# One DMA per channel index over all 128 partitions, in place of one DMA per image over 64

## The chip, the cores and the metric

The kernel runs on one core of one Trainium2 chip. The metric is the time of one execution in microseconds (us) on the device. Three executions of the kernel before took 1348.41, 1350.67 and 1353.38 us; their median is 1350.67 us.

## The reference

The input x is float32 of shape (32 images, 384 channels, 64, 64). Each channel group is normalised, displaced by an integer offset that belongs to one of 48 positions (8 channels each), filtered by a 5x5 Gaussian with the fraction of the offset, and added to x:

```python
def _gn(v, G=32, eps=1e-5):          # 32 groups of 12 channels
    g = v.reshape(B_, G, C_ // G, H_, W_)
    return ((g - mean(g)) / sqrt(var(g) + eps)).reshape(v.shape)

off_round = round(offset)             # (48, 2)
disp = displace(x.reshape(B, P, cpp, h, w), off_round)   # zero outside the image
sub = offset - off_round
kernel = exp(-sum((grid + sub)**2) / (2 * 0.5**2)); kernel /= sum(kernel)   # 5x5 for each position
out = depthwise_conv(disp, kernel, padding=2)

x = x + conv_ref(_gn(x), offset)
```

Displacement and filter are separable, so the kernel applies both as two matrix products, one along the rows of an image and one along its columns.

## The kernel before, in words

**Tiles.** A step handles 2 images (B) and 24 channels (SUPER). 16 steps (STEPS) go over the 32 images; 16 superblocks (NSUPER) go over the 384 channels. That is 256 steps of 768 KB each way. A tile `xin[:, s]` has 128 partitions: partition 2*(16*a + m) + b holds lane a (one of 4 channels), four image rows (block m of 16), image b. Its free axis has 6 channel indices q (Q) of 256 elements, 1 KB each. So one image has the even partitions and the other the odd ones. `xin` has 16 slots, one for each step of a superblock.

**Engines in one step t.** SyncE (queue SP) loads x into slot s. VectorE (DVE) takes the statistics ten steps ahead of use (`statistics`, L395), and adds the result into `xin` (`add_x`, L411 and L414). GpSimd (POOL) makes mean and scale. ScalarE (ACT) normalises the tile of step t + 1 into `norm` (two instructions, L498), copies `y` of step t out of PSUM (one instruction, L507), and then issues the store of step t - 2 (L523). TensorE (PE) multiplies along the rows (`yp`, L572), and along the columns one step later (`xp`, L591).

**Order.** Every engine has its own program in a fixed order, and semaphores tie them. On ACT the order is `normalise(t + 1)`, `copy_y(t)`, `store(t - 2)`, and in 5 of the 16 steps of a superblock one more activation behind the store (L476 twice, L480, L487 twice), which prepares the matrices of the next superblock. `copy_y(t)` waits for `y_done`, that is for the last L572 matmul of step t. `y_products(t + 1)` on PE waits for `y_ready`, that is for `copy_y(t)`, since there is one `yp` buffer, and for `norm_ready` of its step. The DMAs of a store are issued by ACT's own sequencer, so they stand in the same program as the activations.

**Loops.** The first and the last superblock are written out; the 14 between them are one hardware loop, whose body is 16 steps. In the loop each DMA is preceded by register work for its address.

**Loads.** SP waits for `stored[s]`, the completion of both DMAs of the store of this slot, and then issues the load of the same slot for the next superblock. Each DMA adds 16 to its semaphore.

Of the kernel before, what the change touches and what calls it, by code (L numbers as in the profile page):

```python
# [11 lines left out]
P = 128  # L12
POSITIONS = 48
B = 2
LANES = 4
R = 4
BLOCKS = HW // R
SUPER = 24
NSUPER = CH // SUPER
Q = SUPER // LANES  # L20
# [23 lines left out]
def displaced_conv(nc: bass.Bass, x: bass.AP, offset: bass.AP, out: bass.AP):  # L44

    def tiled(a):
        return a.rearrange("(m b) (s q a) (h r) w -> m b s (a h) q (r w)", b=B, s=NSUPER, q=Q, a=LANES, r=R)

    x_t, out_t = tiled(x), tiled(out)
    off_row = offset.rearrange("(o p) k -> o (p k)", o=1)  # L50

    with ExitStack() as ctx:
        def sb(name, shape, dt=F32):
            return ctx.enter_context(nc.sbuf_tensor(name, shape, dt))

        def sem(name):
            return ctx.enter_context(nc.semaphore(name))


        xin = sb("xin", [P, SLOTS, Q, ROW])  # L60
# [66 lines left out]
        loaded = [sem(f"loaded{i}") for i in range(SLOTS)]  # L127
        stored = [sem(f"stored{i}") for i in range(SLOTS)]
# [36 lines left out]
        def run(step):  # L165

            def superblock(c, head=False, tail=False):
                for s in range(STEPS):
                    step(c, s, head, tail)
            superblock(0, head=True)  # L170
            with nc_engine[0].Fori(1, NSUPER - 1) as c:
                superblock(c)
            superblock(NSUPER - 1, tail=True)
# [3 lines left out]
        @block.sync  # L177
        def _(sync):
            sync.dma_start(off[:, :, :], off_row.to_broadcast([P, 2 * POSITIONS])).then_inc(off_loaded, 16)

            def load(c, s):
                for b in range(B):
                    sync.dma_start(xin[b:P:B, s], x_t[s, b, c]).then_inc(loaded[s], 16)

            for s in range(SLOTS):
                load(0, s)
            with sync.Fori(1, NSUPER) as c:
                for s in range(SLOTS):
                    sync.wait_ge(stored[s], 16 * B * c)
                    load(c, s)  # L190
            for s in range(SLOTS):
                sync.wait_ge(stored[s], 16 * B * NSUPER)

        @block.gpsimd
        def _(pool):
# [91 lines left out]
        def _(dve):  # L287
# [101 lines left out]

            def statistics(c, s, n, pair=None):  # L390
                if n == 0:
                    dve.wait_ge(loaded[s], 16 * B * (c + 1))
                if pair is not None:
                    dve.wait_ge(stat_summed, pair - 3)
                nc.vector.bn_stats(stats[:, s // 2 % 4, s % 2, n, :],  # L395
                                   xin[:, s].rearrange("p (g q) f -> p q f g", g=GROUPS)[:, n]).then_inc(bn_done, 1)
# [20 lines left out]
            for s in range(QUAD):  # L417
                for part in range(CHUNKS):
                    statistics(0, s, part)
# [6 lines left out]
            for s in range(QUAD, 2 * QUAD):  # L426
                for part in range(CHUNKS):
                    statistics(0, s, part)
            for s in range(2 * QUAD, AHEAD):
                for part in range(CHUNKS):  # L430
                    statistics(0, s, part, pair=4 if part == 0 and s == 2 * QUAD else None)
# [33 lines left out]
        @block.scalar  # L465
        def _(act):
            nc_engine[0] = act
            act.wait_ge(taps_sq, 1)
            nc.scalar.activation(tap_sq[:], tap[:], ACT.Square).then_inc(taps_sq, 1)
            act.wait_ge(taps_sq, 2)  # L470
            nc.scalar.activation(tap_e[:], tap_sq[:], ACT.Exp, scale=-2.0).then_inc(taps_exp, 1)

            def square(c, part):
                source, target = ((t_int, t_isq), (t_full, t_fsq))[part]
                act.wait_ge(dist_ready, 2 * c + part + 1)
                nc.scalar.activation(target[:], source[:], ACT.Square).then_inc(sq_ready, 1)  # L476

            def exponential(c):
                act.wait_ge(sq_ready, 2 * c + 2)
                nc.scalar.activation(t_exp[:], t_fsq[:], ACT.Exp, scale=-2.0).then_inc(exp_ready, 1)  # L480

            def fill_rows(c, part):
                if part == 0:
                    act.wait_ge(made, c + 1)
                    if c is not 0:
                        act.wait_ge(mats_ready, MATS * c)
                nc.scalar.activation(next_ay[:].rearrange("p n r (m b) -> p n (r m) b", b=B)[:, :, :, part],  # L487
                                     t_msk[:, :, 0:R].rearrange("p n r m -> p n (r m)"), ACT.Identity,
                                     scale=same[:, part:part + 1]).then_inc(next_ay_ready, 1)

            def normalise(t, s, quad, g, first):
                if g == 0:
                    act.wait_ge(coef_ready, quad + 1)
                    if not first:
                        act.wait_ge(y_done, t - 1)
                cv, col = s // QUAD % 2, GROUPS * (s % QUAD) + g
                cols = slice(QG * HW * g, QG * HW * (g + 1))
                nc.scalar.activation(norm[:, s % 2, :, cols].rearrange("p r (q w) -> p q r w", w=HW),  # L498
                                     xin[:, s, QG * g:QG * (g + 1)].rearrange("p q (r w) -> p q r w", w=HW),
                                     ACT.Identity, bias=bias[:, cv, col:col + 1],  # L500
                                     scale=rstd[:, cv, col:col + 1]).then_inc(norm_ready, 1)

            def copy_y(t, v, first):
                act.wait_ge(y_done, t + 1)
                if not first:
                    act.wait_ge(x_done, ADDS * (t - 1))
                nc.scalar.activation(y[:, v].rearrange("p k r a m -> p a (k r) m"),  # L507
                                     yp[:, :, 0:POS * P].rearrange("p a (n m) -> p a n m", m=32),
                                     ACT.Copy).then_inc(y_ready, 1)

            square(0, 0)
            square(0, 1)
            exponential(0)
            act.wait_ge(filled, FILLS)
            for part in range(B):
                fill_rows(0, part)
            for g in range(GROUPS):
                normalise(0, 0, 0, g, True)

            def store(c, s, t):  # L520
                act.wait_ge(result_ready, ADDS * (t + 2))
                for b in range(B):
                    act.dma_start(out_t[s, b, c], xin[b:P:B, s]).then_inc(stored[s], 16)  # L523

            def step(c, s, head, tail):
                t = STEPS * c + s
                nxt = (s + 1) % STEPS
                q_next = QUAD * c + (s + 1) // QUAD
                if not (tail and s == STEPS - 1):
                    for g in range(GROUPS):  # L530
                        normalise(t + 1, nxt, q_next, g, head and s == 0)
                copy_y(t, s % 2, head and s <= 1)
                if s >= BEHIND:
                    store(c, s - BEHIND, t - BEHIND)
                elif not head:
                    store(c - 1, s - BEHIND + STEPS, t - BEHIND)
                if not tail:
                    if 4 <= s < 6:
                        square(c + 1, s - 4)
                    if s == 6:  # L540
                        exponential(c + 1)
                    if 10 <= s < 10 + B:
                        fill_rows(c + 1, s - 10)
            run(step)
            for s in range(STEPS - BEHIND, STEPS):
                store(NSUPER - 1, s, TOTAL - STEPS + s)
# [99 lines left out]
```

## Time and profile before

| | |
|---|---|
| median of three executions | 1350.67 us |
| profiled execution, its own time | 1354.66 us |
| its span, first to last instruction | 1352.8 us |
| mean granted clock of TensorE | 0.992 |
| busy: PE, DVE, ACT, POOL | 90%, 73%, 70%, 20% |
| DMA: bytes, packets | 403.14 MB, 409771 |

The profile shows one execution. A busy time counts the work of an engine, not that of its sequencer: register instructions and the issuing of DMAs stand apart, in rows whose engine has a q behind its name (ACTq, SPq). A duration in such a row is the time that the issuing sequencer was held; the data move later, in the 16 DMA engines. A bracket behind a row of the timeline gives the idle time before it and what ended it.

### The profile page before, as it was taken

The page shows a single profiled execution, that of the slowest core. Times are in us where ns is not written, and L with a number is a line of the kernel's source. Part 1 is how long each engine was busy: PE and PEld are TensorE (multiplying, and loading weights), DVE is VectorE, ACT ScalarE, POOL GpSimd, SP SyncE. Part 2 cuts the span into 40 slices and gives each one's busy share as a digit, 9 for nine tenths or more (in the row PEclk, how much of TensorE's full clock was granted, in tenths as well). Part 3 has the DMA queues.
Part 4 walks back from the last instruction along what each step waited for, and adds up shares of the span by engine and source line. Part 5 has one row for each costly group of instructions (what it writes and reads, how often), then busy time and mean ns, then how long its engine had stood idle before and what let it go on. Part 6 is the DMA issues. An engine that isn't in the chain of part 4 may idle for free.

```text
span 1352.8 us, 110317 instructions
## 1 busy us (share of the span) xinstructions
PE 1213.8 (90%) x49408; PEld 1142.0 (84%) x49408; DVE 991.2 (73%) x1530; ACT 942.3 (70%) x851; POOL 274.3 (20%) x646
## 2 busy tenths in 40 slices
PE   0888999999999999999999999999999999999897
PEld 0788888888898888888888888888888888888787
DVE  7667677777777777777777777777777777777543
ACT  3566776767777677776767777677777767777464
POOL 3211222122121211212121222212212122121010
PEclk9989999999999999999999999999999999999899
DMA  9589899999999999999999999999999999999745
GB/s 313 160 265 314 271 309 311 314 314 315 318 301 316 314 316 308 318 307 320 308 313 316 313 311 320 301 324 310 310 320 306 311 313 318 318 311 309 234 164 187
DMA packets 409771, 403.14 MB, mean 298 GB/s; under 512 B 16528, under 2 KB 409744, under 8 KB 409744
## 3 DMA queue, kind: packets, MB, share of 16 engines
q1 hardware_dynamic: 204944, 201.41, 48.2%
q10 hardware_dynamic: 204800, 201.36, 44.0%
q8 instruction: 18, 0.29, 0.1%
q14 instruction: 9, 0.07, 0.0%
HBM read 201.38 MB, written 201.33 MB: 298 GB/s over the span
## 4 chain that ended last, share of the span: by engine, by line
PE 89%; issue 7%; DVE 2%; ACT 0%; POOL 0%; ACTq 0%; POOLq 0%; DVEq 0%
PE yp L572 56%; PE xp L591 29%; PE xp L557 4%; DVE stats L395 1%; ACT y L507 0%; DVE xin L414 0%; ACT norm L498 0%; ACT next_ay L487 0%; POOL grid_i L200 0%; ACTq L523 0%; DVE t_msk L372 0%; DVE ay L382 0%; DVE tap_sum L358 0%; DVE tap_inv L361 0%; DVE sub L338 0%
## 5 line engine op out<-in xcount | busy, mean ns | idle before, releaser
L572 PE MATMUL yp<-ay,norm 32*128 32x128 f32 x24576 | 766.4, 276 | 66.8 <-ACT y L507 44.8
L572 PEld LDWEIGHTS yp<-ay,norm 32*128 32x128 f32 x24576 | 718.1, 188 | 89.9 <-issue 82.4
L507 ACT ACTIVATE y<-yp 128x1536 f32<-128x1536 f32 x256 | 371.5, 1451 | 310.5 <-PE yp L572 310.3
L498 ACT ACTIVATE norm<-xin,bias,rstd 128x768 f32<-128x768 f32 x512 | 496.9, 1018 | 53.4 <-issue 43.3
L395 DVE BATCH_NORM_STATS2 stats<-xin 128x6 f32<-128x512 f32 x768 | 508.4, 692 | 0.0
L591 PE MATMUL xp<-ax,y 64*64 64x64 f32 x24576 | 421.0, 221 | 9.6 <-issue 8.8
L591 PEld LDWEIGHTS xp<-ax,y 64*64 64x64 f32 x24576 | 384.8, 135 | 41.5 <-issue 10.9
L411 DVE TENSOR_TENSOR xin<-xp,xin 128x512 f32<-128x512 f32 x256 | 176.9, 691 | 321.6 <-PE xp L591 321.6
L414 DVE TENSOR_TENSOR xin<-xp,xin 128x1024 f32<-128x1024 f32 x256 | 309.4, 1208 | 12.2 <-PE xp L591 12.2
L241 POOL TENSOR_TENSOR stats<-stats 128x12 f32<-128x12 f32 x128 | 27.0, 211 | 986.6 <-DVE stats L395 980.0
L258 POOL TENSOR_TENSOR rstd<-var,mhalf 128x8 f32<-128x8 f32 x64 | 104.9, 1639 | 5.0
L557 PE MATMUL xp<-stats,ones 128*128 (+1 forms) x256 | 53.2, 292 | 56.4 <-POOL stats L241 29.0
L557 PEld LDWEIGHTS xp<-stats,ones 128*128 128x128 f32 x256 | 39.1, 192 | 73.1 <-issue 59.1
L487 ACT ACTIVATE next_ay<-t_msk,same 128x768 f32<-128x768 f32 x32 | 32.4, 1017 | 13.6 <-issue 7.7
L220 POOL TENSOR_TENSOR t_int<-grid,place 128x960 f32<-128x960 f32 x16 | 28.7, 1796 | 7.0 <-DVEq L354 7.0
L226 POOL TENSOR_TENSOR t_full<-t_int,sub 128x960 f32<-128x960 f32 x16 | 28.7, 1796 | 2.5 <-POOL t_int L220 2.3
L403 DVE TENSOR_REDUCE both<-xp 128x12 f32<-128x36 f32 x128 | 23.8, 186 | 4.9 <-PE xp L557 4.9
L382 DVE COPY ay<-next_ay 128x512 f32<-128x512 f32 x48 | 17.5, 422 | 12.2 <-PE yp L572 11.2
L476 ACT ACTIVATE t_isq<-t_int 128x960 f32<-128x960 f32 x16 | 16.1, 1004 | 8.1 <-issue 5.8
L476 ACT ACTIVATE t_fsq<-t_full 128x960 f32<-128x960 f32 x16 | 16.1, 1003 | 4.6 <-issue 3.7
L372 DVE SCALAR_TENSOR_TENSOR t_msk<-t_isq,t_exp 128x960 f32<-128x960 f32 x16 | 18.4, 1149 | 0.0
L480 ACT ACTIVATE t_exp<-t_fsq 128x960 f32<-128x960 f32 x16 | 16.0, 1003 | 2.9 <-issue 2.8
(52 smaller groups left out, 105.9 us busy)
## 6 DMA issues: line engine op xcount, KB each, us to landing
xin<-in_x_dram SPq DMA_DIRECT2D x512, 384.0 KB, 5.4
out_dram<-xin ACTq DMA_DIRECT2D x512, 384.0 KB, 4.2
off<-in_L_conv_offset_dram SPq DMA_DIRECT2D x1, 48.0 KB, 3.2
```

Source lines behind the costliest of these rows:

```text
L220: pool.tensor_tensor(t_int[:], grid[:, None, :, :].to_broadcast([P, POS, KINDS, HW]), place[:, bass.ds(POS * c, POS), :].unsqueeze(3).to_b ...
L258: pool.tensor_tensor(rstd[:, v], var[:, v], mhalf[:, :], ALU.pow).then_inc(small, 1)
L395: nc.vector.bn_stats(stats[:, s // 2 % 4, s % 2, n, :], xin[:, s].rearrange("p (g q) f -> p q f g", g=GROUPS)[:, n]).then_inc(bn_done, 1)
L411: nc.vector.tensor_tensor(at, xp[:, 2:4, 0], at, ALU.add).then_inc(result_ready, 1)
L414: nc.vector.tensor_tensor(at, xp[:, 0:2], at, ALU.add).then_inc(result_ready, 1)
L476: nc.scalar.activation(target[:], source[:], ACT.Square).then_inc(sq_ready, 1)
L487: nc.scalar.activation(next_ay[:].rearrange("p n r (m b) -> p n (r m) b", b=B)[:, :, :, part], t_msk[:, :, 0:R].rearrange("p n r m -> p n ...
L498: nc.scalar.activation(norm[:, s % 2, :, cols].rearrange("p r (q w) -> p q r w", w=HW), xin[:, s, QG * g:QG * (g + 1)].rearrange("p q (r w ...
L507: nc.scalar.activation(y[:, v].rearrange("p k r a m -> p a (k r) m"), yp[:, :, 0:POS * P].rearrange("p a (n m) -> p a n m", m=32), ACT.Cop ...
L557: nc.tensor.matmul(xp[:, 3, 1, 0:2 * GROUPS * 9], ones[:, :], stats[:, bass.ds(j, 1)].rearrange("p v t g s -> p (v t g s)"), start=True, s ...
L572: last = nc.tensor.matmul(yp[:, a, P * k:P * (k + 1)], norm[rows, v, r, P * k:P * (k + 1)], ay[rows, k, r, :], start=(r == 0), stop=(r == ...
L591: last = nc.tensor.matmul(xp[outs, 2 * (k // 2) + h, k % 2, HW * r:HW * (r + 1)], y[rows, v, k, r].rearrange("p a m -> p (a m)")[:, outs], ...
```

## The change

Each step's load and store is cut along the channel index q instead of the image b. Before there were two DMAs, each of one image: 64 partitions by 6 channel indices by 1 KB (384 KB, 384 rows of 1 KB). Now there are six DMAs, each of one channel index: 128 partitions by 1 KB (128 KB, 128 rows of 1 KB). The bytes, the size of a row and the slots stay the same. The semaphore counts follow: `stored` and `loaded` rise by 16 * 6 for each step instead of 16 * 2.

```diff
     def tiled(a):
-        return a.rearrange("(m b) (s q a) (h r) w -> m b s (a h) q (r w)", b=B, s=NSUPER, q=Q, a=LANES, r=R)
+        return a.rearrange("(m b) (s q a) (h r) w -> m s q (a h) b (r w)", b=B, s=NSUPER, q=Q, a=LANES, r=R)
...
             def load(c, s):
-                for b in range(B):
-                    sync.dma_start(xin[b:P:B, s], x_t[s, b, c]).then_inc(loaded[s], 16)
+                for q in range(Q):
+                    sync.dma_start(xin[:, s, q], x_t[s, c, q]).then_inc(loaded[s], 16)
...
-                    sync.wait_ge(stored[s], 16 * B * c)
+                    sync.wait_ge(stored[s], 16 * Q * c)
...
-                    dve.wait_ge(loaded[s], 16 * B * (c + 1))
+                    dve.wait_ge(loaded[s], 16 * Q * (c + 1))
...
             def store(c, s, t):
                 act.wait_ge(result_ready, ADDS * (t + 2))
-                for b in range(B):
-                    act.dma_start(out_t[s, b, c], xin[b:P:B, s]).then_inc(stored[s], 16)
+                for q in range(Q):
+                    act.dma_start(out_t[s, c, q], xin[:, s, q]).then_inc(stored[s], 16)
```

On ACT, in steps 4 and 5 of the first superblock, the program before has two DMAs of shape 64x6x256 between the copy of `y` and the activations that follow:

```order
L507 ACTIVATE y<-yp 128x4x12x32
L523 DMA out_dram<-xin 64x6x256 x2
L476 ACTIVATE t_isq<-t_int 128x960
L498 ACTIVATE norm<-xin,bias,rstd 128x3x4x64 x2
L507 ACTIVATE y<-yp 128x4x12x32
L523 DMA out_dram<-xin 64x6x256 x2
L476 ACTIVATE t_fsq<-t_full 128x960
```

At the same place the changed program has six of shape 64x2x256:

```order
L507 ACTIVATE y<-yp 128x4x12x32
L523 DMA out_dram<-xin 64x2x256 x6
L476 ACTIVATE t_isq<-t_int 128x960
L498 ACTIVATE norm<-xin,bias,rstd 128x3x4x64 x2
L507 ACTIVATE y<-yp 128x4x12x32
L523 DMA out_dram<-xin 64x2x256 x6
L476 ACTIVATE t_fsq<-t_full 128x960
```

No activation moved against another; each `norm` pair now stands behind four more issues.

On SP, the start of the program and of its loop, before and now (ISA is the register work of an address; the first of them also holds the wait for the slot):

```order
 L179 DMA off<-in_L_conv_offset_dram 128x96
-L183 DMA xin<-in_x_dram 64x6x256 x32
+L183 DMA xin<-in_x_dram 128x1x256 x96
 L187 UNCONDITIONAL_BRANCH
 L187 ISA
 L183 ISA
```

The 16 first loads are 96 DMAs instead of 32. In both loops, SP's and ACT's, each of the added DMAs brings an ISA row of its own. PE's and DVE's programs are the same row for row.

## Rows read from the trace of the kernel before

**Rows 1.** The page, part 1: busy time of each engine.

```profile
PE 1213.8 (90%) x49408; PEld 1142.0 (84%) x49408; DVE 991.2 (73%) x1530; ACT 942.3 (70%) x851; POOL 274.3 (20%) x646
```

**Rows 2.** The page, part 4: the chain that ended last, by engine.

```profile
PE 89%; issue 7%; DVE 2%; ACT 0%; POOL 0%; ACTq 0%; POOLq 0%; DVEq 0%
```

**Rows 3.** Waits, whole span: us in total, times, longest us.

```profile
ACT y L507 <- PE yp L572: 310.3, 255, 14.0
...
PE yp L572 <- ACT y L507: 44.8, 110, 1.2
```

**Rows 4.** Timeline, a plain step: start us, us, engine, line, what.

```profile
600.83 1.45 ACT L507 ACTIVATE y<-yp 128x1536 f32<-128x1536 f32 x1 [1.26 <-PE yp L572]
...
602.61 1.95 ACT L498 ACTIVATE norm<-xin,bias,rstd 128x768 f32<-128x768 f32 x2 [0.32 <-issue]
...
602.66 2.96 PE L572 MATMUL yp<-ay,norm 32*128 32x128 f32 x96 [0.33 <-ACT y L507]
...
603.54 3.74 SPq L183 DMA_DIRECT2D xin<-in_x_dram  x4
...
605.68 1.45 ACT L507 ACTIVATE y<-yp 128x1536 f32<-128x1536 f32 x1 [1.12 <-PE yp L572]
605.89 1.59 ACTq L523 DMA_DIRECT2D out_dram<-xin  x2
```

**Rows 5.** Timeline of ACT alone, a step with an extra activation.

```profile
641.23 1.45 ACT L507 ACTIVATE y<-yp 128x1536 f32<-128x1536 f32 x1 [0.36 <-PE yp L572]
641.44 1.39 ACTq L523 DMA_DIRECT2D out_dram<-xin  x2
642.95 1.00 ACT L476 ACTIVATE t_fsq<-t_full 128x960 f32<-128x960 f32 x1 [0.26 <-issue]
643.86 1.93 ACT L498 ACTIVATE norm<-xin,bias,rstd 128x768 f32<-128x768 f32 x2
646.08 1.45 ACT L507 ACTIVATE y<-yp 128x1536 f32<-128x1536 f32 x1 [0.29 <-PE yp L572]
```

**Rows 6.** Timeline of ACT: the same `y` copy in two successive superblocks.

```profile
616.51 1.45 ACT L507 ACTIVATE y<-yp 128x1536 f32<-128x1536 f32 x1 [1.73 <-PE yp L572]
...
696.96 1.45 ACT L507 ACTIVATE y<-yp 128x1536 f32<-128x1536 f32 x1 [1.74 <-PE yp L572]
```

**Rows 7.** Line L523 alone: duration ns min/median/max, first and last start.

```profile
L523 ACTq DMA_DIRECT2D out_dram<-xin x512: 607/616/1662, 52.0 to 1348.6; - x171
L523 ACTq FUSED_REGOPS  x448: 37/37/65, 128.4 to 1255.2; - x150
L523 ACTq MOVE out_dram<-xin x448: 29/29/41, 128.5 to 1255.3; - x150
```

**Rows 8.** Lines L183 and L179 alone, the same columns.

```profile
L183 SPq DMA_DIRECT2D xin<-in_x_dram x512: 604/605/2146, 1.2 to 1276.8; - x171
...
L179 SPq DMA_DIRECT2D off<-in_L_conv_offset_dram x1: 397/397/397, 0.7 to 0.7; - x1
```

**Rows 9.** The page, part 6: KB each, median us from issue to landing.

```profile
xin<-in_x_dram SPq DMA_DIRECT2D x512, 384.0 KB, 5.4
out_dram<-xin ACTq DMA_DIRECT2D x512, 384.0 KB, 4.2
```

**Rows 10.** The page, parts 2 and 3: DMA packets, and the queues' shares.

```profile
DMA packets 409771, 403.14 MB, mean 298 GB/s; under 512 B 16528, under 2 KB 409744, under 8 KB 409744
...
q1 hardware_dynamic: 204944, 201.41, 48.2%
q10 hardware_dynamic: 204800, 201.36, 44.0%
```

**Rows 11.** Timeline, the start and the end of the span.

```profile
11.57 7.32 DVE L395 BATCH_NORM_STATS2 stats<-xin 128x6 f32<-128x512 f32 x12
...
1345.37 3.88 ACTq L523 DMA_DIRECT2D out_dram<-xin  x4
...
1346.70 1.23 DVE L414 TENSOR_TENSOR xin<-xp,xin 128x1024 f32<-128x1024 f32 x1 [0.77 <-PE xp L591]
```

**Rows 12.** The chain in order of time, superblock 0: start us, us, what.

```profile
83.73 2.98 issue
```

More of the change, by code:

```diff
@@ L188, in _ @@
                 for s in range(SLOTS):
-                    sync.wait_ge(stored[s], 16 * B * c)
+                    sync.wait_ge(stored[s], 16 * Q * c)
                     load(c, s)
             for s in range(SLOTS):
-                sync.wait_ge(stored[s], 16 * B * NSUPER)
+                sync.wait_ge(stored[s], 16 * Q * NSUPER)
         @block.gpsimd
```

## The prediction

> **What bounds the kernel now.** I read the busy times first. PE is busy 90% of the span, DVE 73%, ACT 70% [rows 1], so PE is the candidate. The chain that ended last agrees: 89% of it is PE, and the queue of ACT, which issues the stores, has 0% [rows 2]. Then the waits: ACT waits 310.3 us for PE's `yp` matmuls before its copies of `y`, and PE waits back for ACT only 44.8 us [rows 3]. So PE sets the pace, and ACT has slack in each step.
>
> How much slack is told by the timeline of one plain step [rows 4]. The copy of `y` starts at 600.83. The two `norm` activations of the next step start at 602.61 and take 1.95 us, so ACT is through at 604.56. The next copy cannot start before PE is through with its 96 matmuls, at 602.66 + 2.96 = 605.62, and starts at 605.68. ACT idles 1.12 us. In a step with an extra activation only 0.29 us is left, before the copy at 646.08 [rows 5]. Between the same copy in two superblocks lie 696.96 - 616.51 = 80.45 us for 16 steps, 5.03 us a step [rows 6]; the loop has 14 such superblocks.
>
> What fills the time between a copy and the next `norm` is the issuing of the store. In rows 5 the copy starts at 641.23, the first DMA is issued from 641.44 and the second is issued until 642.83, and only then, at 642.95, does the next activation start. The copy itself runs meanwhile: ACT's sequencer passes an activation on and goes to the next instruction, but a DMA holds it for some 616 ns [rows 7]. The two are 1.39 us, so 1.39 - 2 x 0.616 = 0.16 us lies between them, which is the register work in front of each (37 and 29 ns, once for each of the 448 DMAs of the loop, [rows 7]).
>
> **The change, part by part.** The bytes and the 1 KB rows are the same. What grows is the count of issues: 6 in place of 2 for each load and each store. PE and DVE keep their programs.
>
> *Price of an issue.* The trace has no DMA of 128 rows of 1 KB. It has DMAs of 384 rows at 605 ns on SP and 616 ns on ACT [rows 7, 8], and one of 128 rows, of 384 bytes each, at 397 ns [rows 8]. If the time goes by the count of rows, the new one costs 0.40 us. If it is a fixed price of one instruction, it costs 0.616 us. Below these, the price could be proportional to the rows: 0.616/3 = 0.205 us. The 397 ns row has the same number of rows and is the nearest. But its pattern in memory is simpler than 64x2x256, it is on SP (11 ns cheaper), and it ran alone, while two ACT issues beside SP's took 1.59 us instead of 1.39 [rows 4, 5]: 0.1 us for each at worst, and both queues will issue more. I take 0.45 us.
>
> *ACT's chain, from the dispatch of a copy to the next copy.* 0.21 us to the first issue, six issues at 0.45 = 2.70, five gaps of 0.16 = 0.80, 0.12 us from the last issue to the first `norm` (642.83 to 642.95), and the two `norm` at 0.92 us each from start to start (642.95 to 643.86 is one such distance) = 1.84. The sum is A = 5.67 us. With an extra activation it is 6.59. Today's A is 0.21 + 1.39 + 0.12 + 1.84 = 3.56, or 4.48 with the extra one, below 5.03.
>
> *PE's chain* B, from the start of a copy to the moment at which the next may be passed on: today's 5.03 us on average, since today the copies wait for nothing else.
>
> *How they combine.* When the copy is passed on while `norm` still runs, it starts late, but the sequencer already issues the next store. With D the dispatch and T the start of copy k, T(k+1) = D(k) + A and D(k+1) = T(k) + B. Two steps then take A + B, one step (A + B)/2. For 16 steps of which 5 have the extra activation, A sums to 16 x 5.67 + 5 x 0.92 = 95.3 us and B to 80.45. Half of the sum is 87.9 us, 7.4 us more than today. That times 14 is +104 us.
>
> *First and last superblock.* There the gaps between issues have no register work (about 0.05 us). A is then 0.55 us less, 5.1, against B of 4.6 to 5: about +0.1 a step, some 3 us, and +0.45 for each of the 5 extra activations, some 2 us. I take +4 for both.
>
> *Start.* SP issues 24 DMAs before slot 3 is full: 24 x 0.5 = 12 us, and landing takes 5.4 us at most [rows 9]. Slot 3 is wanted by DVE at 11.57 + 3/4 of 7.32 = 17.1 us [rows 11]. This is about a tie: 0 to +2, I take 0.
>
> *End.* The last four issues take 3.88 us from 1345.37, partly waiting for the last addition, which ends at 1347.93 [rows 11]. After it six issues of 0.5 us stand where two of 0.64 stood, +1.7 us; the last DMA is a third of the size, so it lands sooner. I take +1.
>
> *SP in the loop.* Six issues and their register work, 6 x (0.45 + 0.18) = 3.8 us, lie beside a step of 5.5 us. A slot is stored two steps after its use and read by DVE four steps later, 22 us. Of that go 3.5 us for issuing and 4.2 for landing of the store, 3.8 and 5.4 for the load [rows 9], 17 us. It stays hidden; with SP at 0.605 us it does too (4.7 us).
>
> *DMA engines.* They are 92.2% busy [rows 10], 1247 us, or 48.7 ns a packet over 16 engines. Of packets under 512 bytes there are 16528, which is 16 for each of the 1025 DMAs and 128 for the offsets. The change adds 16 x 2048 = 32768 of them. Even at the price of a full packet that is 100 us more, 1347 us in all, below what ACT asks for. So cost nothing, covered by ACT's own lateness.
>
> *Sum.* 104 + 4 + 0 + 1 = +109 us on the profiled execution's 1354.66 us gives 1463. That execution was 4 us above the median of 1350.67, so against the median it is 1459 us.
>
> **Rivals.**
>
> *Fixed price of an issue.* An issue stays at 0.616 us. For it: loads and stores of 384 rows hardly vary, 604/605 and 607/616 ns. Against it: the 397 ns row. A = 6.67, sum 111.3, half of (111.3 + 80.45) is 95.9, +15.4 a superblock, +216 in the loop and some +10 at the ends: 1577 us.
>
> *No running ahead.* The sequencer doesn't pass the copy on while `norm` is under way, so a step costs A alone: 95.3 a superblock, +14.9 x 14 = +208, and +6: 1565 us. For it: in the trace no copy is ever passed on late, ACT waits for PE 255 times of 256 [rows 3]. Against it: the second `norm` starts 0.92 us after the first, though one takes over 1 us.
>
> *The loop's code no longer stays resident.* Each of the 64 added DMAs of a loop body brings three instructions (rows 7 show the two beside it), 192 in 16 steps on ACT. If the jump back then has to fetch, the price nearest in the trace is PE's stall of 2.98 us while its program moves on to new code [rows 12]. On ACT it lies in the chain that is now late, and some three quarters of it count: 14 x 2.3 = +32 us, 1491 us. Nothing in this trace shows ACT fetching in its loop, whose copies follow each other at the same distances in each superblock. The Trainium skill, Runtime: NRT & Kernel Launch, section Instruction fetch mechanics, says that an engine other than PE holds two blocks of 256 instructions, and that a jump to a block outside them stalls. By that rule ACT's old body fits and the new one, 192 longer, may not; the sum would be the rival's. No row here shows such a stall on ACT.
>
> *Not slower.* The issue goes in proportion to the rows, 0.205 us. A is 4.2, with the extra activation 5.1, so the 11 plain steps stay under 5.03 and the 5 others lose 0.05 each: +4 us in the loop, 1355 us. The point from which it decides: A passes B = 5.03 at an issue of 0.34 us in plain steps. Against it: the 397 ns row is above that.
>
> **How the numbers follow.** The forecast (an issue of 0.40 to 0.52 us, which gives 1425 to 1508 us) has 45%. Fixed price 12%, no running ahead 10%, code fetch 20%, not slower 5%; 8% for an issue between 0.25 and 0.40 us. The predicted time is 1459 us. The range of 1395 to 1570 us takes in the fetch rival and the one without running ahead, and leaves out the fixed price in part and the case that is not slower. A measurement here can tell about 0.5% (7 us) from no change. Slower by more than that holds in all cases but one: 94%; within it 4%; faster 2%, since nothing on PE's chain gets shorter.
>
> **What the profile after would show.** Right: the median of the L523 issue between 0.40 and 0.52 us; six of them from 0.2 us after each copy, and the `norm` starting some 3.8 us after the copy; the copies of `y` waiting for PE far less than 310 us, and PE waiting for ACT some 100 us more than 44.8; superblocks of about 88 us with copies alternately early and late; PE's busy time as before. SP would still wait for stores. Wrong: issues over 0.6 us; or a gap of some microseconds once in a superblock, at the jump; or superblocks still at 80.5 us, or DVE waiting for loads.

## The result: 1.20 times as long, and the profile after

The changed kernel takes 1618.31 us (median of four, 1610.74 to 1622.55) against 1351.68 us: the ratio is 1.197, with a 95% interval of 1.192 to 1.202. The forecast was 1459 us in a range up to 1570. The direction was right; the loss is 267 us and not 108.

The profiled execution has a span of 1618.0 us. These are its busy times and then the chain that ended last, to be held against [rows 1] and [rows 2]:

```profile
PE 1272.4 (79%) x49408; PEld 1194.8 (74%) x49408; DVE 993.0 (61%) x1530; ACT 917.6 (57%) x851; POOL 274.1 (17%) x646
...
ACTq 53%; issue 20%; ACT 12%; PE 11%; SPq 2%; DVE 0%; DMA 0%
```

The bound has passed from PE to ACT. ACT is busy for less of the span than before and still leads the chain, because what leads it is ACTq: the sequencer while it issues DMAs. An engine's busy share does not show that. The waits of the changed kernel, in the columns of [rows 3], turned round with it:

```profile
ACT norm L498 <- issue: 447.6, 171, 6.3
...
PE yp L572 <- ACT y L507: 257.9, 189, 4.1
...
ACT y L507 <- PE yp L572: 56.7, 34, 19.6
```

ACT's wait for PE fell from 310.3 to 56.7 us, and PE's for ACT rose from 44.8 to 257.9. The issues of the store and of the load (columns as in [rows 7], [rows 8]):

```profile
L523 ACTq DMA_DIRECT2D out_dram<-xin x1536: 546/554/2299, 60.0 to 1615.0; - x192
```

```profile
L183 SPq DMA_DIRECT2D xin<-in_x_dram x1536: 537/538/1533, 1.2 to 1535.6; - x192
```

An issue of 128 rows takes 554 ns where one of 384 rows took 616. So there are three times the issues at nearly the same price. The timeline of ACT alone shows two steps of the loop, to be held against [rows 5]:

```profile
805.34 1.44 ACT L507 ACTIVATE y<-yp 128x1536 f32<-128x1536 f32 x1
805.37 4.10 ACTq L523 DMA_DIRECT2D out_dram<-xin  x6
809.58 1.03 ACT L498 ACTIVATE norm<-xin,bias,rstd 128x768 f32<-128x768 f32 x1 [2.80 <-issue]
810.41 0.55 ACTq L523 DMA_DIRECT2D out_dram<-xin  x1
810.51 1.01 ACT L498 ACTIVATE norm<-xin,bias,rstd 128x768 f32<-128x768 f32 x1
811.12 0.55 ACTq L523 DMA_DIRECT2D out_dram<-xin  x1
811.43 1.42 ACT L507 ACTIVATE y<-yp 128x1536 f32<-128x1536 f32 x1
```

The six issues hold the sequencer for 4.10 us, and the engine stands idle for 2.80 of them before `norm`. The row at 810.41 is worth a second look: it is the first DMA of the next store, and it is issued before the second `norm` starts (810.51) and a microsecond before the copy that precedes it in the program (811.43). So the sequencer has passed `norm` and the copy on and runs ahead, as the forecast's recurrence wanted.

A superblock is now 97.8 us: the same copy stands at 148.02 and, 14 superblocks later, at 1517.49. Before, it stood at 128.31 and 1259.55, 80.8 us each.

```profile
148.02 1.43 ACT L507 ACTIVATE y<-yp 128x1536 f32<-128x1536 f32 x1
...
1517.49 1.43 ACT L507 ACTIVATE y<-yp 128x1536 f32<-128x1536 f32 x1
```

Of the 265 us of span, 238 are in those 14 superblocks. The others are the start (the first copy at 50.52 and not 42.77, +7.7), the first superblock (97.5 and not 85.5, +12) and the stretch behind 1517.49 (100.5 and not 93.3, +7).

One place in each superblock is unlike the rest, the jump at the end of ACT's loop body:

```profile
922.68 2.75 ACTq L523 DMA_DIRECT2D out_dram<-xin  x4
929.51 1.95 ACT L498 ACTIVATE norm<-xin,bias,rstd 128x768 f32<-128x768 f32 x2 [5.74 <-issue]
931.37 1.43 ACT L507 ACTIVATE y<-yp 128x1536 f32<-128x1536 f32 x1
```

The last issue ends at 925.43, and the `norm` starts 4.1 us later, where 0.12 us is usual. Before, ACT's next instruction started 0.24 us after the start of the branch, at each of the 13 jumps; now it starts 2.96 to 3.80 us after it. The profile of the changed kernel has a trace of why, in one of the queues that bring instructions (packets, MB, share), which had 9 packets and 0.07 MB before:

```profile
q14 instruction: 91, 0.75, 0.2%
```

The stall has an echo on PE. It idles 3.82 us, the granted clock in the stretch from 929 to 938 us is 0.62 on average (1.00 from 938 to 945 us), so part of the stretch is at 1.2 GHz and not at 2.4, and the 96 matmuls of the next `yp` take 5.33 us where [rows 4] has 2.96:

```profile
932.93 5.33 PE L572 MATMUL yp<-ay,norm 32*128 32x128 f32 x96 [3.82 <-ACT y L507]
```

### The profile page after: what moved, and what is told of

It is laid out like the page before. It is cut to its first block, busy times and chain, and to the rows that moved or that the text cites. A ratio compares the mean times of both kernels' runs of the same rounds, so it can differ in the third digit from the quotient of the medians.

```text
span 1618.0 us, 116077 instructions
## 1 busy us (share of the span) xinstructions
PE 1272.4 (79%) x49408; PEld 1194.8 (74%) x49408; DVE 993.0 (61%) x1530; ACT 917.6 (57%) x851; POOL 274.1 (17%) x646
## 4 chain that ended last, share of the span: by engine, by line
ACTq 53%; issue 20%; ACT 12%; PE 11%; SPq 2%; DVE 0%; DMA 0%
ACTq L523 52%; PE yp L572 10%; ACT norm L498 7%; ACT y L507 5%; SPq L183 2%; PE xp L591 1%; ACTq L521 0%; ACTq L506 0%; ACTq L495 0%; DMA xin<-in_x_dram 0%; DVE xin L414 0%; ACTq L504 0%; DVE stats L395 0%; ACTq L171 0%; PE xp L557 0%
## 5 line engine op out<-in xcount | busy, mean ns | idle before, releaser
L572 PE MATMUL yp<-ay,norm 32*128 32x128 f32 x24576 | 819.0, 288 | 263.6 <-ACT y L507 257.9
L572 PEld LDWEIGHTS yp<-ay,norm 32*128 32x128 f32 x24576 | 769.8, 200 | 291.3 <-issue 287.1
L507 ACT ACTIVATE y<-yp 128x1536 f32<-128x1536 f32 x256 | 366.3, 1431 | 56.9 <-PE yp L572 56.7
```

The lines of the kernel that those rows point to most:

```text
L572: last = nc.tensor.matmul(yp[:, a, P * k:P * (k + 1)], norm[rows, v, r, P * k:P * (k + 1)], ay[rows, k, r, :], start=(r == 0), stop=(r == ...
```

## The experiments

Each ratio is against the kernel before, executed beside the run.

| kernel | us, median | ratio (95%) |
|---|---|---|
| six loads, two stores | 1396.26 | 1.032 (1.030 to 1.034) |
| two loads, six stores | 1624.36 | 1.202 (1.194 to 1.210) |
| four each way, by image | 1442.31 | 1.068 (1.062 to 1.074) |
| six each way, by image | 1687.33 | 1.245 (1.238 to 1.251) |
| before, 20 idle increments in 11 steps | 1401.33 | 1.033 (1.030 to 1.037) |
| before, 11 of them | 1407.59 | 1.038 (1.034 to 1.042) |
| before, 5 of them | 1354.99 | 1.001 (0.999 to 1.003) |
| changed, ACT without a loop | 1529.58 | 1.127 (1.121 to 1.133) |
| changed, issues split three and three | 1447.64 | 1.070 (1.067 to 1.073) |
| both of these | 1376.21 | 1.017 (1.012 to 1.021) |
| six loads by image, two stores | 1429.24 | 1.056 (1.051 to 1.061) |

**Which half of the change.** First the stores go back to two, `stored` counting 16 * B:

```diff
-                for q in range(Q):
-                    act.dma_start(out_t[s, c, q], xin[:, s, q]).then_inc(stored[s], 16)
+                for b in range(B):
+                    act.dma_start(out_t[s, b, c], xin[b:P:B, s]).then_inc(stored[s], 16)
```

> Six loads per step by channel index as in the change, but the two stores by image as before. Theory (ACT's in-order program pays for the issues of the stores, at 0.55 to 0.58 us each): ACT's chain is as before, so 1351 to 1365 us; SP's six issues (some 4.2 us a step) stay hidden, only the start loses about 2 us. Rival (the transfers themselves are worse: more completions, smaller DMAs, loads landing late): a good part of the 267 us stays, 1420 us or more, and DVE waits for loads.

Measured: 1396.26 us. The stores carry most of the loss, but the theory missed by 31 us: the six loads alone cost 44. The waits and the chain name the place:

```profile
ACT y L510 <- PE yp L575: 342.4, 254, 18.3
DVE stats L398 <- DMA xin<-in_x_dram: 216.8, 160, 2.7
```

```profile
SPq L186 <- DMA out_dram<-xin: 1.6, 2, 0.8
```

```profile
SPq 72%; issue 13%; PE 13%; DMA 1%; DVE 0%; ACT 0%; ACTq 0%; DVEq 0%
```

ACT is as free as before. DVE waits 216.8 us for loads, and SP, which waited 852.9 us for stores before, waits 1.6: it issues without a pause and is the bound. Alone an issue takes 538 ns and 0.18 us of register work, 4.3 us for six, which would fit into 5.03. But its mean between 200 and 1100 us is 683 ns, and those with no ACT issue beside them are held longest (0.775 us in the mean, one in ten over 1.3 us; the others 0.582). Six times 0.683 + 0.184 is 5.2 us, 83.2 us a superblock; the trace has 83.6. What holds them is not shown. The DMA engines are 94% busy from 200 to 1100 us, but they were 97% busy in the same stretch before the change, where the mean issue of a load was 0.622 us.

The counterpart leaves the loads at two and makes the stores six.

> Six stores per step by channel index, the two loads by image as before. Theory: nearly the whole loss, 1590 to 1620 us, a little less than the changed kernel since fewer issues of SP stand beside ACT's; superblocks of 95 to 98 us; a stall of about 3 us at ACT's jump. Rival (loads and stores share the loss): about 1480 us.

Measured: 1624.36 us, as the changed kernel within the noise, and 4 us above the range of the theory. So the six loads cost almost nothing in the loop while ACT is late; at the start they do, where the first copy is at 43.44 us here and at 50.52 in the changed kernel.

**Count or pattern.** The cut by image is kept and made finer, with `PARTS` 2 and then 3; the loads are cut in the same way as the stores shown here:

```diff
                 for b in range(B):
-                    act.dma_start(out_t[s, b, c], xin[b:P:B, s]).then_inc(stored[s], 16)
+                    for n in range(PARTS):
+                        act.dma_start(out_t[s, b, c, n], xin[b:P:B, s, PER * n:PER * (n + 1)]).then_inc(stored[s], 16)
```

> Four DMAs per step each way, each of one image and three channel indices (64 partitions, 192 rows of 1 KB). Theory: A = 0.21 + 4 x 0.57 + 3 x 0.16 + 0.12 + 1.84 = 4.93 us in plain steps, just under PE's 5.03, and 5.85 in the five others, so 1375 to 1395 us, and no stall at the jump if ACT's loop still stays resident. Rival (the loss is in proportion to the count of DMAs): halfway, 1485 us.

> Six DMAs per step each way as in the change, but each of one image and two channel indices (64 partitions, 128 rows of 1 KB). Theory (count alone decides): as the changed kernel, 1590 to 1630 us, an issue of 0.54 to 0.56 us. Rival (the pattern over 128 partitions with two images costs): an issue of about 0.4 us as that of the offsets, and 1400 to 1440 us.

Measured: 1442.31 and 1687.33 us. The first missed its range by 47 us: with four issues the body of ACT's loop has 320 instructions, and there is already a stall at each of the 13 jumps, of 3.2 to 5.5 us. The second lies above the ranges of both the theory and the rival and is slower than the changed kernel itself. Its issue, and that of the kernel with four:

```profile
L528 ACTq DMA_DIRECT2D out_dram<-xin x1536: 607/616/2082, 59.9 to 1681.9; - x192
```

```profile
L528 ACTq DMA_DIRECT2D out_dram<-xin x1024: 607/616/1840, 52.7 to 1439.0; - x171
```

The median is 616 ns with 384, 192 and 128 rows of one image alike. So the number of rows has no part in the price here; the pattern has, and the change's own pattern is the cheaper one (554).

**The stall at the jump.** The kernel before, with instructions that do nothing, placed where ACT's sequencer waits for PE anyway:

```diff
+                if not head and not tail and s not in (5, 6, 7, 11, 12):
+                    for _ in range(20):
+                        act.sem_inc(padding, 1)
                 copy_y(t, s % 2, head and s <= 1)
```

> The kernel before, with 20 semaphore increments that nobody waits for added to ACT's program in 11 of the 16 steps of the loop, where its sequencer would wait for PE anyway: the loop body grows by 220 instructions, by as much as the change made it grow and more. Theory (a body that no longer stays resident stalls at the jump back): a gap of about 3 us behind each of the 13 jumps, partly hidden by ACT's slack there, and 1370 to 1400 us. Rival (the gap in the changed kernel has another cause, such as ACT's queue being late): no gap, 1351 to 1360 us.

> The same with 11 increments in place of 20 in each of these steps: the body grows by 121 instructions, to about 345. Theory: it still stays resident, the jump takes 0.25 us as before, and 1349 to 1356 us. Rival (what costs is the executing of the added instructions): about half of what the 20 increments cost.

> The kernel before with 5 idle semaphore increments in 11 of 16 steps of ACT's loop: the body is 279 instructions long. Bodies of 224 did not stall at the jump, of 320 and more did. If the place of the body's end decides (it would end where SP's loop of 291 ends, which does not stall), no gap and 1350 to 1356 us. If ACT stalls for any body over 256 instructions, a gap of 3 to 6 us and about 1400 us.

Measured: 1401.33, 1407.59 and 1354.99 us. The first is 1 us above its range. The one with 11 refutes what I expected of it, and helps more by that: it executes about half as many increments and loses as much. With 5 the loss is gone. So what costs isn't the executing. The body of ACT's loop, counted in the trace from jump to jump, has 224 instructions before, 279 with 5 increments, 345 with 11 and 444 with 20; the next instruction starts 0.24 us after the branch in the first two and 3.8 to 6.5 us after it in the others. The queue that brings instructions goes with it, first with 5 increments and then with 11:

```profile
q14 instruction: 9, 0.07, 0.0%
```

```profile
q14 instruction: 75, 0.61, 0.1%
```

ACT with 11 increments, at a jump:

```profile
714.47 1.45 ACT L508 ACTIVATE y<-yp 128x1536 f32<-128x1536 f32 x1 [1.01 <-PE yp L576]
714.69 1.43 ACTq L524 DMA_DIRECT2D out_dram<-xin  x2
721.10 1.95 ACT L499 ACTIVATE norm<-xin,bias,rstd 128x768 f32<-128x768 f32 x2 [5.18 <-POOL bias L261]
```

The row blames GpSimd's `bias`, but the branch stands between the last issue, through at 716.12, and the `norm`; the releaser is only the last of the semaphores. The loss of 53 us with 11 increments is 4.1 for each of the 13 jumps, that of 47 us with 20 is 3.6.

Which bodies stall is shown, but the rule behind it is not. Bodies of 224 and 279 instructions on ACT and of 291 on SP (in the changed kernel) do not stall; those of 320, 345, 416 and 444 on ACT do. A limit of length between 291 and 320 would fit, and so would a limit on where the body ends: counted from the first instruction of each engine in the trace, the former end at 405 or earlier and the latter at 471 or later. No run here separates the two. The Trainium skill, Runtime: NRT & Kernel Launch, section Instruction fetch mechanics, says that two blocks of 256 instructions are held and that a taken branch to a place outside them has to wait for a fetch. It agrees with these traces if some 41 to 72 more instructions stand ahead of ACT's first in the trace, an estimate from the places of the bodies that no run here shows.

**The changed kernel without the jump.** ACT's 14 superblocks are written out:

```diff
-            with nc_engine[0].Fori(1, NSUPER - 1) as c:
-                superblock(c)
+            if unrolled:
+                for c in range(1, NSUPER - 1):
+                    superblock(c)
+            else:
+                with nc_engine[0].Fori(1, NSUPER - 1) as c:
+                    superblock(c)
...
-            run(step)
+            run(step, unrolled=True)
```

> The changed kernel with ACT's program written out for all 256 steps, without a loop. Theory: no jump, so no stall of 3 us, and no register work between the issues (gaps of 0.05 us in place of 0.16): A = 5.7 and 6.6 us, superblocks of 88 to 89 us, 1455 to 1475 us. Rival (neither jump nor register work matters, the issues alone do): above 1550 us.

Measured: 1529.58 us, 91.9 us a superblock instead of 97.8. It missed its range by 55 us. Without the register work the gaps between issues are 0.03 us in place of 0.16, and the first issue follows a copy by 0.01 us in place of 0.21. But the median issue grew from 554 to 637 ns; why issues that come closer together take longer is not shown. With the mean of this trace, 0.658 us, A is 0.01 + 6 x 0.658 + 5 x 0.03 + 0.12 + 1.84 = 6.07 us, its sum over 16 steps is 101.7, and half of that and 80.45 is 91.1. So the recurrence fits within 0.8 us, and the price of an issue was the miss.

```profile
L527 ACTq DMA_DIRECT2D out_dram<-xin x1536: 546/637/2080, 60.4 to 1531.3; - x192
```

**The same issues in another place.** Three behind the copy, three behind the `norm` pair of the next step:

```diff
+                rest = BEHIND + 1
+                if s >= rest:
+                    store(c, s - rest, t - rest, 1)
...
                 copy_y(t, s % 2, head and s <= 1)
                 if s >= BEHIND:
-                    store(c, s - BEHIND, t - BEHIND)
+                    store(c, s - BEHIND, t - BEHIND, 0)
```

> The changed kernel with each store's six issues split on ACT: three behind the copy of y, three behind the norm pair of the next step, before the next copy. The same DMAs, the same count. Theory (what costs is that norm stands behind six issues): norm is dispatched after three issues, the sequencer's own total of 5.0 to 5.2 us a step becomes the bound, superblocks of 82 to 84 us and the stall at the jump on top, 1400 to 1450 us. Rival (the total time of issuing decides, wherever it stands): as the changed kernel, 1600 us.

Measured: 1447.64 us, within the range of the theory. Of the 267 us, 171 are gone with all 1536 issues still on ACT. A step of it:

```profile
805.02 1.29 ACTq L524 DMA_DIRECT2D out_dram<-xin  x2
806.36 1.01 ACT L487 ACTIVATE next_ay<-t_msk,same 128x768 f32<-128x768 f32 x1 [0.62 <-issue]
806.61 0.55 ACTq L524 DMA_DIRECT2D out_dram<-xin  x1
807.26 1.01 ACT L498 ACTIVATE norm<-xin,bias,rstd 128x768 f32<-128x768 f32 x1
807.32 1.34 ACTq L524 DMA_DIRECT2D out_dram<-xin  x2
```

The issues now run beside the activations and no longer ahead of them. Away from the jump the steps take 4.8 to 5.3 us on average, as before the change.

Both cures together:

> The changed kernel with the six issues of a store split three and three around the norm pair, and with ACT's program written out without a loop. Theory (place of the issues and the jump are the two halves of what is left): ACT is no longer the bound; what is left is SP's six issues beside a DMA queue that holds them back, as with six loads and two stores (83.4 us a superblock), so 1385 to 1410 us. If the loads can keep up, 1355 to 1370 us. Rival (six issues on ACT cost something wherever they stand): above 1430 us.

Measured: 1376.21 us, 81.7 us a superblock, and the chain is PE's again:

```profile
PE 87%; issue 7%; SPq 3%; ACT 1%; ACTq 1%; DVE 0%; DMA 0%
```

That is under the range expected of late loads and over that of loads that keep up. Of the 24 us left over the kernel before, 7 are the start, 4 the first superblock and 14 x 0.9 = 13 the others. Nothing tried here beats the kernel before; it is bound by PE, and hardly any issue of a DMA is on that path.

The loads are a surprise here. Beside two stores of 384 KB each, the six loads of a step were held (0.683 us in the mean) and set the pace at 83.6 us a superblock. Beside six stores of 128 KB the same six loads take 0.552 us in the mean, DVE waits only 7.3 us for them, and a superblock takes 81.7 us. So it is not the six loads by themselves that are slow.

**What makes an issue dear.** Loads of nine shapes are added behind the end of the work, each alone. The edit in part:

```diff
+            def probe(dst, src):
+                sync.dma_start(dst, src).then_inc(probed, 16)
+                k[0] += 1
+                sync.wait_ge(probed, 16 * k[0])
```

> The kernel before, with 18 loads of nine shapes added behind everything else at the end of SP's program, each waited for before the next, so that each issue is measured alone (the output is untouched; the span grows by some 50 us). Runs so far: 64x6x256, 64x3x256 and 64x2x256 by image take 605 ns on SP, 128 partitions by one index 538, the offsets 397. Theory 1 (the price goes by the dimensions that the pattern still has on each side, and not by rows): about 0.40 us for the flat ones (128x256, 128x96, 64x256, 128x1536), 0.54 where one side has one more, 0.605 where both have, and no difference between 64x2x256 and 64x6x256. Theory 2 (a price for each row and for each byte): 128x256 costs as much as 128x1x256 by two images, 0.54, and 128x1536 much more.

One execution of 1409.38 us, each shape twice. Five rows of the second round, in the order 128x256 flat, 128x1x256 from two images, 64x256, 64x6x256, 128x6x256:

```profile
1380.72 0.34 SPq L199 DMA_DIRECT2D xin<-in_x_dram  x1
...
1387.31 0.55 SPq L199 DMA_DIRECT2D xin<-in_x_dram  x1
...
1389.69 0.50 SPq L199 DMA_DIRECT2D xin<-in_x_dram  x1
...
1394.19 0.61 SPq L199 DMA_DIRECT2D xin<-in_x_dram  x1
...
1401.99 0.38 SPq L199 DMA_DIRECT2D xin<-in_x_dram  x1
```

64x2x256 took 0.61 too, 128x96 and 128x1536 both 0.33. The load of the offsets, 397 ns at the start of the program, took 0.33 here as well. Theory 2 falls: neither rows nor bytes count, 768 KB cost as little as 48 KB. Theory 1 is half right: flat patterns over 128 partitions are cheap, but 128x6x256, which has one more dimension on both sides, costs 0.38, and the flat 64x256 costs 0.50. All that are dear have a leading count of 64 on one side or both. Those with 64 partitions also take only every second partition, so which of the two features counts is open.

**Loads by image.** Six loads of 64x2x256 a step, two stores:

```diff
                 for b in range(B):
-                    sync.dma_start(xin[b:P:B, s], x_t[s, b, c]).then_inc(loaded[s], 16)
+                    for n in range(PARTS):
+                        sync.dma_start(xin[b:P:B, s, PER * n:PER * (n + 1)], x_t[s, b, c, n]).then_inc(loaded[s], 16)
```

> Six loads per step, each of one image and two channel indices, two stores as before. With six loads by channel index and two stores the time was 1396 us, with loads that arrived late. If the number of loads decides, SP's issue is now 605 ns and not 538, six of them with their register work take 6 x 0.785 = 4.7 us, and the time is 1396 us or more. If it is the pattern over all partitions that makes those loads slow in the DMA engines, these are not late and the time is 1352 to 1360 us.

Measured: 1429.24 us, above the kernel with six loads by channel index (1396.26). SP's mean issue is 0.704 us; six with their register work are 5.3 us. So it is not that a transfer spans all partitions that makes the six loads late. What the six cost by their number is less clear: at their undisturbed 0.605 us they would take 4.7 us and fit into 5.03, and what holds them longer is open here too.

## Why the prediction was wrong

**What bounded the kernel before, and where the cost would lie:** right. The loss stands on ACT's sequencer behind the copy of `y`, and with ACT out of the way the chain is PE's again, at 1376 us.

**PE's busy time as before:** wrong, though it was to be a sign of being right. It rose by 59 us, from 1213.8 to 1272.4, 53 of them in the same `yp` matmuls, whose rows here are before and after (busy us, mean ns, idle us before them):

```profile
L572 PE MATMUL yp<-ay,norm 32*128 32x128 f32 x24576 | 766.4, 276 | 66.8 <-ACT y L507 44.8
```

```profile
L572 PE MATMUL yp<-ay,norm 32*128 32x128 f32 x24576 | 819.0, 288 | 263.6 <-ACT y L507 257.9
```

Not only the jumps do this. In 38 of the 256 steps the 96 matmuls take over 3.1 us, against 8 steps before, and in 31 steps of the kernel that has no jump on ACT. A place far from a jump, where the mean granted clock from 875.2 to 880 us is 0.64, so partly at 1.2 GHz:

```profile
875.27 4.42 PE L572 MATMUL yp<-ay,norm 32*128 32x128 f32 x96 [2.05 <-ACT y L507]
```

So a late ACT also makes PE slower in some steps, and the forecast's B of 5.03 us had nothing of that. How much of it reaches the time was not measured.

**The price of an issue:** the term that was mis-sized. It was taken as 0.45 us, near the 397 ns of the offsets' load, because that row had the same number of rows. The measured median is 0.554 us and the mean 0.578 from 200 to 1100 us. The row count was the wrong likeness: with 384, 192 and 128 rows of one image the price stayed 616, and the offsets' own load took 397 ns once and 328 ns twice in the probe. The dearer rows of [rows 7, 8], both with a leading 64 as the new pattern has on its HBM side, were the nearer ones. With 0.578, A is 6.4 and 7.3 us in place of 5.67 and 6.59, A over 16 steps is 107.3, and half of it and B's 80.45 is 93.9 where the forecast had 87.9: 6 us a superblock, 84 us in all.

**How the chains combine:** right. The sequencer does run ahead, so the rival without it falls; the copies come alternately early and late (805.34, 811.43, 816.55, 822.71 us); and splitting the issues, which this mechanism said would help, took away 171 us.

**The code that no longer stays resident:** a rival with 20%, and it came true on top of the dearer issue. Its price was 2.3 us a superblock, from a stall of 2.98, counted for 14 jumps where there are 13. Measured on the kernel before, with increments added, it is 3.6 to 4.1 for each jump, PE's slower product behind the gap included, of which the forecast had nothing. 93.9 + 3.6 to 4.1 gives 97.5 to 98.0 us a superblock; the trace has 97.8. That sum uses a jump's price from another kernel and leaves out PE's slower steps away from the jump, so the agreement is better than its terms deserve.

**Start and ends:** +5 was forecast, +27 came. At the start only slot 3 was looked at. PE's first product also comes behind the statistics of the slots up to 7, and there the loads are late:

```profile
34.82 1.90 DVE L395 BATCH_NORM_STATS2 stats<-xin 128x6 f32<-128x512 f32 x3 [1.05 <-DMA xin<-in_x_dram]
...
38.47 1.90 DVE L395 BATCH_NORM_STATS2 stats<-xin 128x6 f32<-128x512 f32 x3 [1.76 <-DMA xin<-in_x_dram]
...
42.27 1.89 DVE L395 BATCH_NORM_STATS2 stats<-xin 128x6 f32<-128x512 f32 x3 [1.90 <-DMA xin<-in_x_dram]
```

An issue is 0.65 us from start to start there, 31 us for the 48 of eight slots. The first copy is 7.7 us late, and the first superblock pays the dearer issues too. So the forecast fell short by 84 us for the issue's price, by some 50 for the jump, and by 22 at the start and the ends, of 159 in all.

**SP and the DMA engines hidden:** right for this kernel, and not in general. Beside ACT as it was, six loads a step bound the kernel at 1396 us. The working had taken the issue at 0.45 us, or 0.605 at worst; the mean was 0.683 there, and why some issues are held for over a microsecond stays open.

**The other rivals.** The fixed price was nearly true (0.554 of 0.616), and its 1577 us were nearest to the result, though partly by luck: it had neither the jump nor the late start. With 0.616 and the jump, 95.9 + 4.1 = 100 us a superblock, one comes near the six DMAs each way by image (102.5). It deserved more than 12%: its rows were on the same engines, with the same leading count, and were there over a thousand times, against one. "Not slower" had nothing for it.

## What to carry to other kernels

The issue of a DMA held its engine for 0.33 to 0.61 us when alone, and 48 KB held it as long as 768 KB. So on an engine that also computes, count the issues and look at what stands behind them in program order; the busy share of the engine shows nothing of it. If they can't be fewer, spread them between the activations: the same 1536 issues cost 171 us less that way. And when instructions are added to a loop, ask whether the body still fits where it fitted before, since the jump back can cost more than they do.

## What the runs showed of the hardware

- The price of an issue went by the pattern and neither by rows nor by bytes: on SP, alone, 0.33 us for 128x96, 128x256 and 128x1536, 0.38 for 128x6x256, 0.50 for 64x256, 0.55 to 0.59 for 128x1x256 against 64x2x256, 0.61 for 64x2x256 and 64x6x256.
- Issues of SP and ACT overlap and hold each other only a little: at 6 and 6 a step, ACT's take 0.569 us in the mean with none of SP's beside them and 0.581 with one. But ACT's own at closer distance (gaps of 0.03 us in place of 0.16) take longer, 637 ns in the median for 554.
- A loop body of 224 or 279 instructions on ACT jumps back in 0.24 us, one of 320 to 444 in 3 to 6.5 us, with 9 packets in its instruction queue for the whole program in the one case and 75 to 91 in the other.
- PE came back from 3.8 us of idleness behind such a jump partly at the lower clock: 5.33 us for 96 matmuls that take 2.96. Behind 2.05 us of idleness it was 4.42 us.
- Still open: what holds SP's issues for over a microsecond when six loads stand beside two stores. The DMA engines are 94% busy there, 97% before the change, and beside six stores the same loads are not held.
